# Causal attention on one core: score products, row-maximum units and output products in a written-out order, two output steps at a time in the second half of the queries

## The reference

```python
qkv = jnp.einsum('bsd,ndh->bnsh', x, W_qkv)
q, k, v = jnp.split(qkv, 3, axis=-1)
attn = jnp.einsum('bnqh,bnkh->bnqk', q, k) * scale
mask = -10000000000.0 * (1.0 - jnp.tril(jnp.ones((S, S))))
attn = jax.nn.softmax(attn + mask, axis=-1)
out = jnp.einsum('bnqk,bnkh->bnqh', attn, v)
...
x = _layernorm(x + attention, axis=-1)
```

## Time and profile before

| | |
|---|---|
| Time, median of 3 runs | 1630.11 us (1629.15 to 1633.2) |
| Profiled execution: its own time, and span of its instructions | 1630.98 us, 1629.0 us |
| PE busy | 1497.6 us (92%) |
| DVE busy | 1099.3 us (67%) |
| ACT busy | 953.6 us (59%) |
| POOL busy | 446.8 us (27%) |
| Mean granted TensorE clock | 0.961 of full |

### The profile page before, as it was taken

How to read it: one execution, slowest core, us unless ns; L and a number is a source line. 1 busy time by engine, 2 the same in 40 slices (tenths; PEclk the granted TensorE clock), 3 DMA queues, 4 the chain that set the end, 5 groups by cost and what they waited for, 6 DMA issues and landing times. The chain is left out here.

```text
span 1629.0 us, 30478 instructions
## 1 busy us (share of the span) xinstructions
PE 1497.6 (92%) x9050; PEld 726.0 (45%) x9050; DVE 1099.3 (67%) x1749; ACT 953.6 (59%) x2103; POOL 446.8 (27%) x563
## 2 busy tenths in 40 slices
PE   5979988999998998998998998999998999999995
PEld 3546533343343343343333333433423566656664
DVE  3212258778776776776776776777752688878875
ACT  3536521767666766766766666676676455545442
POOL 5424310111123213212213313313324262222222
PEclk9989976999999999999999999999999999999998
DMA  4887771123363373382382373374371532101001
GB/s 133 265 279 250 262 228 29 58 58 114 99 113 87 96 148 85 96 160 76 99 160 72 109 156 69 94 167 79 91 115 50 112 75 92 45 21 52 26 27 39
DMA packets 166778, 178.57 MB, mean 110 GB/s; under 512 B 26397, under 2 KB 135784, under 8 KB 166632
## 3 DMA queue, kind: packets, MB, share of 16 engines
q1 hardware_dynamic: 166632, 176.70, 42.4%
HBM read 109.79 MB, written 66.06 MB: 108 GB/s over the span
## 5 line engine op out<-in xcount | busy, mean ns | idle before, releaser
L784 DVE TENSOR_REDUCE a_mx<-a_ps_m 128x1 f32<-128x640 f32 (+6 forms) x704 | 700.0, 1027 | 234.2 <-PE a_ps_m L857 233.5
L764 ACT ACTIVATE a_probs<-a_ps_s 128x512 f32<-128x512 f32 (+3 forms) x1536 | 641.2, 498 | 307.5 <-PE a_ps_s L911 300.5
L852 PE MATMUL a_ps_m<-s_ks,s_qs 96*128 96x512 bf16 (+3 forms) x1536 | 396.9, 343 | 38.2 <-DVE a_mx L784 24.7
L911 PE MATMUL a_ps_s<-s_qs,s_ks 99*128 99x512 bf16 (+3 forms) x1536 | 388.7, 332 | 27.0 <-issue 16.9
L719 POOL TENSOR_SCALAR_AFFINE_SELECT a_probs<-a_probs 128x512 f32<-128x512 f32 x256 | 163.2, 637 | 733.9 <-ACT a_probs L764 733.9
L887 PE MATMUL a_ps_o<-a_probs,s_vq 128*32 128x512 f32 (+3 forms) x3072 | 329.6, 501 | 0.7 <-POOL a_probs L719 0.7
L852 PEld LDWEIGHTS a_ps_m<-s_ks,s_qs 96*128 96x128 bf16 x1536 | 127.5, 100 | 295.9 <-DVE a_mx L784 143.2
L911 PEld LDWEIGHTS a_ps_s<-s_qs,s_ks 99*128 99x128 bf16 x1536 | 127.8, 98 | 193.8 <-ACT a_probs L764 102.0
L857 PE MATMUL a_ps_m<-s_mask,s_ident 128*128 128x128 bf16 (+2 forms) x864 | 206.2, 239 | 0.0
L1395 PE MATMUL f_ps_o<-f_w,f_hm 128*128 128x256 f32 (+1 forms) x640 | 152.4, 386 | 0.9 <-DVE f_y L1302 0.9
L226 DVE TENSOR_TENSOR p_rest<-p_ps_qk,h_space 128x512 f32<-128x512 f32 x64 | 44.2, 691 | 154.8 <-ACT h_space L251 154.8
(11 more groups left out here) (120 smaller groups left out, 1132.9 us busy)
## 6 DMA issues: line engine op xcount, KB each, us to landing
qk_parts<-h_space SPq DMA_DIRECT2D x64, 384.0 KB, 2.9
s_qs<-qk_parts SPq DMA_DIRECT2D x192, 128.0 KB, 2.8
s_ks<-qk_parts SPq DMA_DIRECT2D x192, 128.0 KB, 2.8
v_rows<-h_space SPq DMA_DIRECT2D x16, 896.0 KB, 5.4
s_vq<-v_rows SPq DMA_DIRECT2D x32, 448.0 KB, 4.0
f_x_in<-in_L_attn_x_dram SPq DMA_DIRECT2D x16, 512.0 KB, 6.2
heads_out<-a_o_sb SPq DMA_DIRECT2D x128, 64.0 KB
f_x_in<-in_L_attn_x_dram SPq DMA_DIRECT2D x8, 1024.0 KB, 8.6
```

The lines of the kernel that those rows point to most:

```text
L764: act.activation(probs[:, st % PB, h, 0:width], ps_s[:, n % BANKS, 0:width], ACT.Exp, scale=SCALE).then_inc(exps[h % 2], 1)
L784: dve.tensor_reduce(mx[:, e, heads[0]:heads[-1] + 1, qt], span(i), AX_X, ALU.max)\
L852: last = pe.matmul(out, qs[0:TROWS, j, h, q], ks[0:TROWS, j, h, s:s + wide], start=k == 0, stop=mask is None)
L911: pe.matmul(ps_s[:, n % BANKS, 0:width], ks[0:MROWS, j, h, kt * P:(kt + 1) * P], qs[0:MROWS, j, h, q0:q0 + width], start=True, stop=True)\
```

## The change

It replaces the plan by fixed places. A turn counts its score products n = 0 to 47. `UNIT_AT[i]` is the place of unit i (a whole number: ahead of the outputs at that place; with .5: behind them; both ahead of score product n). `OUT_AT[g]` is the place at which the steps of `GROUPS[g-1]` have their output products. The steps of the first half go one at a time; those of the second half go in pairs, (4, 5), (6, 7), (8, 9) and (10, 11), the last pair at place 5 of the turn after. `PB` goes from 3 to 4. ACT's first copy of `ps_o` moves from behind step 4 to behind step 5. DVE inverts the sums behind unit 2 and its split rather than ahead of unit 2. To make room for the fourth buffer, the tile `aw` leaves `h_space` (the layer norm of the first sequence reads and writes `x1` in place; the feed stage has both its `aw` buffers of its own), and in the projection `x_t` moves into `h_space` and `v_sb` out of it.

```diff
@@ attend_stage
-        COLS = [len(heads) * ((qt + 1) * P + P) for heads, qt in UNITS]
-        WIDTHS = [160 + min(CHUNK, (c + 1) * CHUNK - kt * P) for c, kt in STEPS]
...
-        SHARE = [range(a, b) for a, b in zip([0] + ENDS, ENDS)]
-        PB = 3
+        UNIT_AT = [0, 0.5, 3, 5, 7, 9, 11.5, 14, 17.5, 19.5, 21, 23, 24, 26.5, 28, 30, 32.5, 35, 37.5, 39.5, 41.5, 44.5]
+        OUT_AT = [5, 7, 12, 21, 24, 29, 38, 46]
+        GROUPS = [(st,) for st in range(CT)] + [(st, st + 1) for st in range(CT, NST, 2)]
+        PB = 4
@@ attend_stage, scalar
-                            if st == CT:
+                            if st == CT + 1:
                                 keep_o(t, j % 2, 0, sent_before(b, j))
@@ attend_stage, vector
-                        for st in range(NST):
+                        for i in range(NU):
                             if more:
-                                for i in SHARE[st]:
-                                    take_max(t + 2, j % 2, i)
-                                    if i == TURN:
-                                        split_max(t + 1)
-                            elif after and st == 0:
+                                take_max(t + 2, j % 2, i)
+                            if after and i == TURN:
                                 split_max(t + 1)
-                            if later and j == 2 and st == 0:
+                            if later and j == 2 and i == TURN:
                                 residual.invert(dve, b - 1)
@@ attend_stage, tensor
+                        for n in range(QUAD * NST + 1):
+                            for i in range(NU):
+                                if more and UNIT_AT[i] == n:
+                                    rows(t + 2, jm, i)
...
+                            for g in range(len(GROUPS)):
+                                for st in GROUPS[g - 1]:
+                                    if OUT_AT[g] == n and g:
+                                        products(t, j, st)
+                                    elif OUT_AT[g] == n and before:
+                                        products(t - 1, (j - 1) % QUADS, st)
+                                if OUT_AT[g] == n and 0 < g <= CHUNKS * KC and not after:
+                                    head.transposes(pe, ps_m[:, (g - 1) // RBANKS, (g - 1) % RBANKS, :],
+                                                    (g - 1) // KC, (g - 1) % KC, ident)
+                            for i in range(NU):
+                                if more and UNIT_AT[i] == n + 0.5:
+                                    rows(t + 2, jm, i)
...
+                for st in GROUPS[-1]:
+                    products(SLOTS - 1, QUADS - 1, st)
@@ Head
-        sizes = [TILES * D, TILES * D, KC * (SEQ + 2), KC * SEQ, KC * SEQ]
+        sizes = [TILES * D, KC * (SEQ + 2), KC * SEQ, KC * SEQ]
@@ feed_stage
-        aw = [head.aw, sb("f_aw", [P, TILES, D], F32)[:, :, :]]
+        aw = [sb(f"f_aw{e}", [P, TILES, D], F32)[:, :, :] for e in range(2)]
```

More of the change, by code:

```diff
@@ L446, in sem @@
             return ctx.enter_context(nc.semaphore(name))
[L448 removed]
+        sizes = [TILES * D, KC * (SEQ + 2), KC * SEQ, KC * SEQ]
         self.space = sb("h_space", [P, sum(sizes)])
         ends = [sum(sizes[:i + 1]) for i in range(len(sizes))]
[L451 to L452 removed]
+        x1, x1_t, xm, mixa = (self.space[:, b - a:b] for a, b in zip(sizes, ends))
         self.x1 = x1.rearrange("p (t d) -> p t d", t=TILES)
@@ L902, in turn @@
                             pe.wait_ge(loaded[jm], LOADS * (b + 1 + (j + 2) // QUADS))
-                        for st, (c, kt) in enumerate(STEPS):
+                        for n in range(QUAD * NST + 1):
+                            for i in range(NU):
+                                if more and UNIT_AT[i] == n:
+                                    rows(t + 2, jm, i)
+                            if n == 2 * QUAD and after and not more:
+                                pe.wait_ge(rows_max, NU * SLOTS)
+                                turn_max(t + 1, (j + 1) % 2)
+                            for g in range(len(GROUPS)):
[10 more added lines that the diff above has]
+                                    rows(t + 2, jm, i)
+                            if n == QUAD * NST:
+                                break
+                            st, h = divmod(n, QUAD)
+                            c, kt = STEPS[st]
@@ L904, in turn @@
                             off, width = step_shape(st)
                             q0 = c * CHUNK + off
-                            for h in range(QUAD):
-                                n = QUAD * st + h
-                                if before or n >= BANKS:
-                                    pe.wait_ge(exps[(n - BANKS) % 2], 2 * NST * t + (n - BANKS) // 2 + 1)
-                                pe.matmul(ps_s[:, n % BANKS, 0:width], ks[0:MROWS, j, h, kt * P:(kt + 1) * P],
-                                          qs[0:MROWS, j, h, q0:q0 + width], start=True, stop=True)\
-                                  .then_inc(scores, 1)
-                                if more:
-                                    for i in part(SHARE[st], h):
-                                        rows(t + 2, jm, i)
@@ L917, in turn @@
-                            if st == 1 and after and not more:
-                                pe.wait_ge(rows_max, NU * SLOTS)
-                                turn_max(t + 1, (j + 1) % 2)
-                            if st >= 1:
-                                products(t, j, st - 1)
-                            elif before:
-                                products(t - 1, (j - 1) % QUADS, NST - 1)
-                            if more:
-                                for i in part(SHARE[st], QUAD):
-                                    rows(t + 2, jm, i)
@@ L927, in turn @@
-                            if not after and st < CHUNKS * KC:
-                                head.transposes(pe, ps_m[:, st // RBANKS, st % RBANKS, :], st // KC, st % KC, ident)
+                            if before or n >= BANKS:
+                                pe.wait_ge(exps[(n - BANKS) % 2], 2 * NST * t + (n - BANKS) // 2 + 1)
+                            pe.matmul(ps_s[:, n % BANKS, 0:width], ks[0:MROWS, j, h, kt * P:(kt + 1) * P],
+                                      qs[0:MROWS, j, h, q0:q0 + width], start=True, stop=True)\
+                              .then_inc(scores, 1)
```

23 lines of the change are left out of this document (7 added, 16 removed).

## The result

The changed kernel takes 1589.82 us (median of 4 runs, 1585.97 to 1592.34), against 1630.84 (1629.15 to 1633.2, 4 runs) for the kernel before on the same chip: ratio 0.9745 (95% interval 0.9721 to 0.977). The profiled execution took 1585.97 us, the fastest of the four, so a comparison of the two traces (1630.98 before) has 45 us to account for.

A forecast was written before the change was run, and what follows sets the result against it. TensorE's list of work was taken to bound the unit-making stage, 29.73 us a turn with 28.84 busy. Terms -22 - 24 + 5 + 15 + 1.5 = -24.5 us gave 1606 us; own range 1595 to 1616, 8-in-10 range 1594 to 1620.

The forecast's parts named there:

- Pairs: Second-half outputs: four pairs a turn each save a way in and out, 0.185 us taken; -22 us (-11 to -29).
- The wait for DVE: Unit 5's 0.80 us wait for unit 3's maximum goes, since TensorE's 4.08 us cover DVE's 3.66; -24 us.
- the inversion: In six turns, behind the split, it delays unit 3's maximum: a wait of 0.8 us in each, +5 us.
- New waits for ACT: Scores wait for ACT between places 38 and 46 and at score 27: 0.5 us a turn, +15 us.
- small stops: About 1 us of TensorE's 29.7 us turn before the change, left unplaced when its work was summed.
- The pauses at the loop's round stay: Five TensorE pauses of some 3.4 us, one per round of the loop over sequences, stay; counted at nothing.
- The last two turns: Turns without units at attention's end: ACT idles in a pair and two steps follow the last mask; +1.5 us (0.5 to 3).
- The feed stage: Its transposes move to later places, some 4 us, but stay hidden with 4 us of cover; no cost.
- the exposed join: Rival, chance 0.10: the second step's weights load with the array at rest, 0.11 us a pair, +13 us: 1619.
- ACT as the pace: Rival, chance 0.05: ACT never catches up between pairs, 2.7 us a turn in place of 0.5, +66 us: 1672.
- waits only move: Rival, chance 0.07: new waits for ACT and DVE reach 1.3 us a turn, gain spent: 1630, no change.
- More than I count: Rival, chance 0.08: new waits stay below what the trace shows and switches save 0.24 us: -46 us, 1584.

The follow-up runs named there:

- The kernels written out: Attention loops over sequences written out on all five engines, no branch back: changed kernel 1572.99 us, kernel before 1603.73 us.
- the nine variants above: Follow-up kernels made by editing the changed kernel (output or unit places, first copy, inversion, loops written out, a fifth pair); measured 1553.38 to 1651.7 us.
- the kernel before without a round: Kernel before with its attention loops written out on all five engines, so no branch back: 1603.73 us, ratio 0.9842.
- five pairs: Changed kernel with steps 2 and 3 also paired, inversion first, new unit and output places: 1579.46 us; with loops written out on all engines 1553.38 us.

## Why the prediction was right in direction and wrong in size

The sum had -24.5 us; the medians show -41 and the two traces -45. In the order of the prediction:

- **Pairs, -22.** Right in mechanism: some -27, 0.9 us a turn. A pair saves 0.13 coming out and 0.09 going in, where I had taken 0.185 for both together.
- **The wait for DVE, -24, and the inversion, +5.** Right together: -19 forecast, and the waits for DVE fell by 20.6. From unit 2 to unit 5 TensorE's 4.08 us do cover DVE's 3.66, and 17.8 us went from ordinary turns. In the six turns with an inversion a wait of 0.5 to 0.75 us is there as foretold. But these turns waited already before, 0.54 us for the split and 0.47 for unit 3, so there the waits fell too, from 6.0 us to 3.2. I had charged the new wait to the length of an ordinary turn. Counted against the ordinary turn of each kernel they lost 0.27 before and 0.64 to 0.9 after, 2.4 us in all.
- **New waits for ACT, +15.** They are there, and larger: 0.9 us a turn, 26 us. Three stand where I had put them. TensorE in the kernel after, a start to the next start:

```profile
668.55 0.73 PE L917 MATMUL a_ps_s<-s_qs,s_ks 99*128 99x512 bf16 x2
669.12 0.60 PE L839 MATMUL a_ps_m<-s_ks,s_qs 96*128 96x512 bf16 x2
...
673.42 1.02 PE L917 MATMUL a_ps_s<-s_qs,s_ks 99*128 99x512 bf16 x3
674.28 0.38 PE L839 MATMUL a_ps_m<-s_ks,s_qs 96*128 96x512 bf16 x1
...
679.22 0.75 PE L917 MATMUL a_ps_s<-s_qs,s_ks 99*128 99x256 bf16 x3
679.81 0.38 PE L839 MATMUL a_ps_m<-s_ks,s_qs 96*128 96x256 bf16 x2
```

  Two scores at place 27 take 0.57 us and not 0.43, three before the pair at 38 take 0.86 and not 0.65, three narrow ones 0.59 and not 0.33: 0.6 us in all, where I had 0.5. Another 0.3 us stands where I had none, at scores 10, 15 and 16 (two of 128 columns and the first of 512 in this row take 0.48 and not 0.33):

```profile
662.35 0.65 PE L917 MATMUL a_ps_s<-s_qs,s_ks 99*128 99x128 bf16 x3
662.83 0.49 PE L839 MATMUL a_ps_m<-s_ks,s_qs 96*128 96x512 bf16 x2
```

  Each score that is late here starts 0.06 us behind the end of the exponential three products earlier, so it is ACT that they wait for. None is long enough to stand among the waits; they are read from starts alone.
- **The ordinary turn.** By my terms it should have fallen 1.03 us, to 28.7 (the "28.8 to 29.1" that I gave as a sign does not fit my own sum), and it fell 1.24 to 28.49, some 6 us more over 30 turns. It can be read, to within 0.1 us, from the starts in one ordinary turn of each kernel, that of the earlier trace rows and that shown above. The pairs give 0.9. The wait of unit 5 gives 0.96, as the operations around it are delayed by more than the 0.80 that are listed. Of the "about 1 us" of small stops that I had not placed 0.4 went. The largest of these is behind the outputs of step 3, which take 0.52 us to the next start where 0.36 is normal:

```profile
683.20 0.43 PE L887 MATMUL a_ps_o<-a_probs,s_vq 128*32 128x128 f32 x8
683.72 0.55 PE L852 MATMUL a_ps_m<-s_ks,s_qs 96*128 96x512 bf16 x2
```

  Against this stand the 0.9 for ACT and 0.2 in other new stops. So the stops that I left unplaced were the mis-sized part of this term. With the six turns with an inversion, the turns gave -34.8 where my terms had -26.
- **"The pauses at the loop's round stay." This is the step that failed.** I had costed it at nothing and given no reason. The turn with the round and the one behind it took 34.85 + 29.98 us before and 31.30 + 29.37 after (means of five). Against two ordinary turns of their own kernel that is 5.4 us a round before and 3.7 after: -8.4 us in five rounds. Without it the median would lie inside my range. (So it would without the 8.8 us of the turns, but there the terms were right in kind and off in size.) The earlier trace rows showed the five pauses. What I did not ask is what TensorE had queued when its sequencer began to branch. At the end of the body there stood before a single output step, now there stand a pair and two scores, and they cover 1.5 us of the branch and not 0.6. With them goes a part of the time at the lower clock. The kernels written out bear this out: no pause, no lower clock, and a smaller gain.
- **The last two turns, +1.5.** Right within its range: from the first score of turn 30 to the last outputs are 54.2 us before and 56.5 after, +2.4. The two turns ahead of them fell by 0.7 us more than ordinary ones do. In both kernels one score there waits long for ACT, first before, then after:

```profile
1138.78 0.39 PE L911 MATMUL a_ps_s<-s_qs,s_ks 99*128 99x512 bf16 x1 [1.82 <-ACT a_probs L764]
```

```profile
1098.57 0.82 PE L917 MATMUL a_ps_s<-s_qs,s_ks 99*128 99x512 bf16 x2 [1.42 <-ACT a_probs L754]
```

  TensorE has left its loop by then, but ACT has one round more and is at its own branch, as in the run with TensorE alone written out.
- **The feed stage, nothing.** It took 377.2 us before and 373.1 after, in the two profiled executions. It began at the lower clock before and at the higher after. First the kernel before, then the one after, the same four products behind the same wait:

```profile
1253.10 2.04 PE L1375 MATMUL f_ps_t<-f_row,f_ones 1*128 1x256 f32 x4 [1.27 <-POOL f_ones L1088]
```

```profile
1212.20 1.09 PE L1367 MATMUL f_ps_t<-f_row,f_ones 1*128 1x256 f32 x4 [1.27 <-POOL f_ones L1080]
```

  This is not shown to come from the change: the nine variants above that have the same feed stage as the kernel after took 374.7 to 378.9 us for it, and the kernel before without a round took 373.7. So "nothing" stands, and the profiled execution after had luck here, which the median of the four has not.

These come to -37.2 (30 turns at 1.24), -8.4, +2.4, -0.7, +2.4, and -4.1, with +0.4 for a later first score: -45.2, where the traces have 45.0. Of the 20.5 us that my sum lacked of this, the rounds are 8.4, the turns 8.8 and the feed stage 4.1.

Of the rivals, the exposed join fell by the starts above: the third set follows as the fourth does. The Trainium skill, "TensorE: Matmul & The Clock Gate", Part 3, "The mechanism", says that a weight load overlaps running matmuls only where the row groups differ, and by that sentence the second step's loads would have had to wait; the 0.43 us between sets do not bear it out. The same section also lets a load into the background weight buffer go ahead of running matmuls, and with that the starts agree. ACT as the pace fell too. That waits only move was false for the change and true for its half with the units at their old places. "More than I count" named 1584 and came nearest, but partly by luck: it left out the new waits for ACT, which did come, and it had neither the rounds nor the small stops.

## What to carry to other kernels

A pause that comes once in each round of a loop is a cost of the loop's end as written: look at what the engine has queued when the branch begins, on every engine that loops, and put long work there, or write the loop out on all engines together. Positions of three kinds of work that share one in-order engine don't add: each half of this change alone gave nothing or lost, so a forecast has to be made for the list as a whole. Before charging a new wait to a turn, read that turn's own waits and length in the trace before, not the ordinary one's. And stops too short for a list of waits can add up to 1 us in a turn of 29; the distance from one start to the next shows them.

## What the runs showed of the hardware

- The branch back of a loop holds TensorE's sequencer for about 3.5 us (3578 and 3426 ns in the rows above) and leaves ACT idle for 2.3 to 2.7 us. On TensorE only work already queued ran meanwhile. TensorE ran at its lower clock after each pause of the kernel before (3.2 to 3.7 us) and after three of the five in the kernel after (2.3 to 2.7 us). It also did after the wait of 1.8 us for ACT in the kernel before, and not after that of 1.4 in the kernel after.
- The same turn takes 28.80 us written out and 28.49 in a loop, 29.97 and 29.73 in the kernel before, but 28.03 and 28.01 with five pairs. With TensorE alone written out it is 28.68, so only a part of the difference comes from TensorE's own program. Turns that stand ahead of the loop in the kernel after take 28.7 to 28.8 too. What it is was not found.
- Switching from bf16 products over the whole array to f32 products in four column tiles and back costs 0.09 us in and 0.11 to 0.13 us out. Two steps of the latter with different weights stream on without a gap (sets 0.43 us apart within a step and across the join).
